# A macaron transformer block on one core: another order of work in the two FP4-quantised feed-forward stages

## What is computed

```
x = x + 0.5 * _L0_ffn_ref(_layernorm(x, axis=-1), ...)      # ffn_a
x = x + _L0_attn_ref(_layernorm(x, axis=-1), ...)           # proj_a, attn_a
x = x + 0.5 * _L0_ffn_ref(_layernorm(x, axis=-1), ...)      # ffn_b
x = x + 0.5 * _L1_ffn_ref(_layernorm(x, axis=-1), ...)      # fp4_a
x = x + _L1_attn_ref(_layernorm(x, axis=-1), ...)           # proj_b, attn_b
x = x + 0.5 * _L1_ffn_ref(_layernorm(x, axis=-1), ...)      # fp4_b
```

```
scale = jnp.max(jnp.abs(xb), axis=-1, keepdims=True) / 6.0
xn = xb / scale
idx = jnp.searchsorted(_MID, jnp.abs(xn))
q = _GRID[idx] * jnp.sign(xn) * scale
...
gate = fp4_linear(x, w_gate)
y = fp4_linear(x, w_up)
h = jax.nn.silu(gate) * y
return fp4_linear(h, w_down)
```

## Time and profile before

| | us |
|---|---|
| median of 3 runs | 526.15 |
| lowest, highest | 522.24, 529.05 |
| the profiled execution | 523.24 |
| its span | 521.4 |
| PE busy | 420.8 (81%) |
| DVE busy | 349.1 (67%) |
| POOL busy | 306.6 (59%) |
| ACT busy | 285.9 (55%) |
| granted TensorE clock, mean | 0.91 |

### The profile page before, as it was taken

One profiled execution on the slowest core, in us unless ns is written; L12 is line 12 of the kernel. 1 busy time (PEld: TensorE's weight loads), 2 busy tenths in 40 slices (PEclk: granted clock), 3 DMA queues, 4 the chain that ended last, 5 costly groups with the idle time before them and its releaser, 6 DMA issues. The chain is left out here.

```text
span 521.4 us, 11437 instructions
## 1 busy us (share of the span) xinstructions
PE 420.8 (81%) x3693; PEld 272.6 (52%) x3693; DVE 349.1 (67%) x882; ACT 285.9 (55%) x521; POOL 306.6 (59%) x585
## 2 busy tenths in 40 slices
PE   3997889999999966945677577899999997567766
PEld 1454436666666533523455354677766774235545
DVE  5768686878888527836677755757677773268771
ACT  5774515676666737657664125245554557567631
POOL 5414435777777732356985423456666668589841
PEclk9999858999999989987999689679999999679995
DMA  6002783233331000000000007943333310000001
GB/s 189 2 1 78 181 247 88 73 80 91 94 92 48 3 1 0 2 1 1 0 1 3 0 27 169 257 103 94 94 96 92 92 50 3 0 2 0 21 27 34
DMA packets 31121, 31.77 MB, mean 61 GB/s; under 512 B 4953, under 2 KB 26329, under 8 KB 31074
## 3 DMA queue, kind: packets, MB, share of 16 engines
q1 hardware_dynamic: 31074, 31.18, 22.6%
HBM read 21.30 MB, written 9.44 MB: 59 GB/s over the span
## 5 line engine op out<-in xcount | busy, mean ns | idle before, releaser
L688 ACT ACTIVATE h_sb<-psum 128x1024 f32<-128x1024 f32 (+1 forms) x128 | 110.8, 914 | 53.1 <-PE psum L614 26.9
L729 DVE TENSOR_REDUCE nm<-psum 128x2 f32<-128x512 f32 x128 | 82.3, 685 | 14.1 <-PE psum L594 12.8
L732 DVE TENSOR_REDUCE nm<-psum 128x3 f32<-128x384 f32 x128 | 66.0, 553 | 10.4 <-PE psum L600 8.1
L698 POOL TENSOR_TENSOR h_sb<-h_sb,bandw 128x512 f32<-128x512 f32 x48 | 61.0, 1271 | 0.0
L234 POOL TENSOR_TENSOR rstd<-veps,mhalf 128x4 f32<-128x4 f32 (+1 forms) x32 | 28.4, 889 | 43.2 <-DVE veps L220 41.8
L1029 PE MATMUL psum<-wgT,fxT 128*128 128x352 f32 x64 | 26.8, 547 | 26.6 <-ACT fxT L1094 26.6
L639 PE MATMUL psum<-h_sb,v_b 128*32 128x256 f32 x512 | 43.2, 410 | 4.2 <-POOL h_sb L698 4.1
L702 POOL TENSOR_SCALAR_AFFINE_SELECT h_sb<-h_sb 128x512 f32<-128x512 f32 x64 | 40.8, 638 | 0.0
L766 DVE RECIPROCAL rsum<-psum 128x16 f32<-128x16 f32 x32 | 8.2, 258 | 46.7 <-PE psum L655 46.7
L593 PE MATMUL psum<-kst,qst 72*128 72x256 bf16 x128 | 36.1, 299 | 3.5 <-DVE nm L729 2.7
L594 PE MATMUL psum<-kst,qst 72*128 72x256 bf16 x128 | 36.0, 298 | 0.0
(11 more groups left out here) (234 smaller groups left out, 1167.5 us busy)
## 6 DMA issues: line engine op xcount, KB each, us to landing
qst<-q_dram SPq DMA_DIRECT2D x96, 96.0 KB
kst<-k_dram SPq DMA_DIRECT2D x96, 96.0 KB
q_dram<-q_parts SPq DMA_DIRECT2D x16, 192.0 KB, 2.9
k_dram<-k_parts SPq DMA_DIRECT2D x16, 192.0 KB, 2.9
k_dram<-k_parts SPq DMA_DIRECT2D x16, 128.0 KB, 3.4
x<-in_L_attn_x SPq DMA_DIRECT2D x4, 256.0 KB, 3.9
out_x<-x SPq DMA_DIRECT2D x4, 256.0 KB, 2.3
pk<-in_packed SPq DMA_DIRECT2D x1, 689.5 KB, 5.7
```

The lines of the kernel that those rows point to most:

```text
L688: nc.scalar.activation(pexp[p][:, :, 0:w], psum[:, 4 + 2 * (p % 2):6 + 2 * (p % 2), 0:w], ACT.Exp, scale=scale).then_inc(sem("a_exp"), 1)
L698: ins = nc.gpsimd.tensor_tensor(wide, wide, bandw[:].unsqueeze(1).unsqueeze(1).to_broadcast([P, 2, 2, P]), ALU.mult)
L729: nc.vector.tensor_reduce(nm[slot % 2][:, HEAD[h]], bank[e].rearrange("p (t k) -> p t k", t=2), AX.X, ALU.max, negate=True).then_inc(sem(" ...
L732: nc.vector.tensor_reduce(nm3[slot % 2][:, HEAD[h]], bank[e][:, 0:3 * P].rearrange("p (t k) -> p t k", t=3), AX.X, ALU.max, negate=True).t ...
```

## The change

The same instructions are issued, with the same shapes, in another order. `pe_f` is parted into transpose, gate and up; `act_f` into the copy of the transposed x and silu; `pool_x_round` into three; h itself is parted from `dve_h_scales`. The steps of a unit get other lags: the chain of x runs ahead, h comes at lag 5, the last x at lag 8, so a stage has 16 steps. fp4_a's steps 0 to 3 stand beside ffn_b's steps 3 to 5, its steps 13 to 15 beside proj_b's 0 to 2; fp4_b's steps 0 to 3 stand before the four slots of the last quad. The weights are quantised with units 4, 5 and 6 of ffn_b, that is in its steps 1, 2 and 3. A few waits on semaphores are added where the new order needs one, such as `wait(pool, "xt", u)`.

```diff
             def pool_x_scaled(pool, u, par):
                 pool.wait_ge(sem("xrs"), u + 1)
+                wait(pool, "xt", u)
...
             def dve_body(dve, k, par, there):
-                if there(4):
-                    dve_h_scales(dve, k - 4, par)
-                if there(5):
-                    dve_h_round(dve, k - 5, 1 - par)
-                if there(1):
-                    dve_x_scales(dve, k - 1, 1 - par)
                 if there(0):
                     dve_stats(dve, k, par)
+                if there(2):
+                    dve_x_scales(dve, k - 2, par)
+                if there(5):
+                    dve_h(dve, k - 5)
+                if there(8):
+                    dve_x(dve, k - 8)
+                if there(5):
+                    dve_h_scales(dve, k - 5, 1 - par)
                 if there(6):
-                    dve_x(dve, k - 6)
+                    dve_h_round(dve, k - 6, par)
 
             def pool_body(pool, k, par, there):
-                if there(2):
-                    pool_x_round(pool, k - 2, par)
                 if there(4):
-                    pool_h_scaled(pool, k - 4, par)
-                if there(5):
-                    pool_h_back(pool, k - 5, 1 - par)
-                if there(1):
-                    pool_x_scaled(pool, k - 1, 1 - par)
+                    pool_x_rounded(pool, k - 4)
+                if there(3):
+                    pool_x_scaled(pool, k - 3, 1 - par)
+                if there(4):
+                    pool_x_back(pool, k - 4, par)
+                if there(6):
+                    pool_h_scaled(pool, k - 6, par)
+                if there(7):
+                    pool_h_back(pool, k - 7, 1 - par)
                 if there(0):
                     pool_rstd(pool, k, par)
+                if there(3):
+                    pool_x_shift(pool, k - 3)
...
-                          ("pe", 1): [("a_y", 8), ("a_exp", PR * 16)]}, {4: 0, 6: 1, 7: 2})
+                          ("pe", 1): [("a_y", 8), ("a_exp", PR * 16)]}, {4: 0, 5: 1, 6: 2})
...
             def next_fp4(slot):
-                if slot >= 2:
-                    step(eng, which, fp4_b, slot - 2)
+                step(eng, which, fp4_b, slot)
...
-            both(ffn_b, 3, 6, fp4_a)
+            for k in range(3):
+                step(eng, which, ffn_b, 3 + k)
+                run(fp4_a, (0, 2, 3)[k], (2, 3, 4)[k])
...
-            run(fp4_a, 3, 11)
+            run(fp4_a, 4, 13)
             proj_b["ahead"](eng, which)
-            both(fp4_a, 11, 14, proj_b)
+            both(fp4_a, 13, 16, proj_b)
             entrance(proj_b, attn_b)
             attention(attn_b, next_fp4)
-            run(fp4_b, 2, 14)
+            run(fp4_b, 4, 16)
```

More of the change, by code:

```diff
@@ L1019, in fp4_phase, with pe_x_transpose @@
             tile_blocks = NBX // 2
[L1021 removed]
+            def pe_x_transpose(pe, u, par):
                 pe.wait_ge(sem("xo"), u + 1)
@@ L1026, in pe_f, with pe_gate @@
                 last.then_inc(sem("d_xTps"), 1)
+            def pe_gate(pe, u, par):
                 pe.wait_ge(sem("d_xT"), u + 1)
@@ L1030, in pe_f, with pe_up @@
                 last.then_inc(sem("d_gps"), 1)
+            def pe_up(pe, u, par):
                 wait(pe, "d_h", u)
@@ L1170, in pool_x_scaled, with pool_x_shift, pool_x_rounded, pool_x_back @@
                 pool.wait_ge(sem("xrs"), u + 1)
+                wait(pool, "xt", u)
                 nc.gpsimd.tensor_tensor(blocks(xbuf["v"][:]), xpad[par][:, :, 0:BLK], spread(xbuf["rs"][:], NBX), ALU.mult).then_inc(sem("xv"), 1)
-            def pool_x_round(pool, u, par):
+            def pool_x_shift(pool, u):
                 pool.wait_ge(sem("xM"), u + 1)
+                wait(pool, "xo", u)
                 nc.gpsimd.tensor_tensor(xbuf["t"][:], xbuf["v"][:], xbuf["M"][:], ALU.add).then_inc(sem("xt"), 1)
+            def pool_x_rounded(pool, u):
                 pool.wait_ge(sem("xt"), u + 1)
                 nc.gpsimd.tensor_tensor(xbuf["t"][:], xbuf["t"][:], xbuf["M"][:], ALU.subtract).then_inc(sem("xq"), 1)
+            def pool_x_back(pool, u, par):
                 pool.wait_ge(sem("xq"), u + 1)
@@ L1205, in pool_body @@
                     pool_rstd(pool, k, par)
+                if there(3):
+                    pool_x_shift(pool, k - 3)
             def pe_body(pe, k, par, there):
-                if there(6):
-                    pe_o_transpose(pe, k - 6, par)
-                if there(3):
-                    pe_f(pe, k - 3, 1 - par)
-                if there(6):
-                    pe_o(pe, k - 6, par)
-            def act_body(act, k, par, there):
-                if there(2):
-                    act_x_magic(act, k - 2)
+                if there(5):
+                    pe_up(pe, k - 5, 1 - par)
@@ new lines, in pe_body, with act_body @@
+                if there(4):
+                    pe_x_transpose(pe, k - 4, par)
+                if there(8):
+                    pe_o(pe, k - 8, par)
+                if there(4):
+                    pe_gate(pe, k - 4, par)
+                if there(7):
+                    pe_o_transpose(pe, k - 7, 1 - par)
+            def act_body(act, k, par, there):
+                if there(3):
+                    act_x_magic(act, k - 3)
+                if there(4):
+                    act_x_copied(act, k - 4, par)
+                if there(1):
+                    act_center(act, k - 1, 1 - par)
+                if there(2):
+                    act_x_six(act, k - 2)
+                if there(6):
+                    act_h_square(act, k - 6, par)
@@ L1218, in act_body @@
                 if there(1):
                     act_scale(act, k - 1, 1 - par)
-                if there(6):
-                    act_o(act, k - 6, par)
-                if there(3):
-                    act_f(act, k - 3, 1 - par)
                 if there(4):
-                    act_h_square(act, k - 4, par)
-                if there(1):
-                    act_x_six(act, k - 1)
-                if there(0):
-                    act_center(act, k, par)
+                    act_silu(act, k - 4)
@@ L1231, in fp4_phase @@
+                if there(7):
+                    act_o(act, k - 7, 1 - par)
             return dict(pe=pe_body, act=act_body, dve=dve_body, pool=pool_body, first=d0, n=8, entry=entry)
@@ L1395, in both @@
                 for k in range(lo, hi):
-                    if ph is not fp4_a or k < 13 or which != "dve":
+                    if ph is not fp4_a or k < 15 or which != "dve":
                         step(eng, which, ph, k)
```

17 lines of the change are left out of this document (9 added, 8 removed).

## The result

| | before | after |
|---|---|---|
| median, us | 527.49 (4 runs) | 507.96 (4 runs) |
| lowest, highest | 522.24, 529.05 | 505.34, 509.61 |
| profiled execution, its span | 523.24, 521.4 | 506.44, 504.6 |
| PE, DVE, ACT, POOL busy in it | 420.8, 349.1, 285.9, 306.6 | 418.7, 350.3, 285.1, 305.0 |
| granted clock, mean | 0.91 | 0.91 |

The ratio is 0.965, with an interval from 0.960 to 0.971: the kernel is faster by 3.5%. The forecast was 509 us for the median and 506.0 for the profiled execution. Busy times are the same within 2.1 us on every engine, so nearly all of the 16.8 us came out of waits. Medians are over all executions of a kernel; every ratio, and a second median where one stands in brackets, leaves out those more than 1.5% above their kernel's fastest.

The account below looks back on a forecast made before the run. Bound: ACT standing still during gate, then PE waiting for ACT. Terms: -8.2 us up to the scores, -9.0 after, so 523.24 profiled becomes 506.0 (0.967), median 509; own range 504 to 514, outer 502 to 519.

Parts of the forecast that it names:

- The ring: Old quantised-stage round: ACT stands still during gate, then PE waits for nearly a round of ACT's work; 6.49 us end to end.
- k = 8 to 10: New rounds of a quantised stage in which POOL, without rstd work, closes the round: 5.25 us.
- The full round: Round k = 7, once a stage, closed by POOL with all its operations: 6.16 us.
- The ring of 4.88: Rounds k = 11 and 12: POOL's h_back, DVE's reduce, reciprocal, scale and roundings, then the next h_back; 4.88 us.
- The weights: ffn_b: weight quantising moved to steps 1 to 3 stalls step 2, +3.1 us; four ready x steps leave gate(0) 0.9 later.
- Attention: Last quad, with fp4_b's steps 0 to 3: attention ends 3.8 us later (bounds 1.2 and 5), gate(0) only 2.1 later.
- The joint: First stage into proj_b: first transposes at 289.4, x(6) 298.0, x(7) 307.4, first scores 317.0 against 325.25, -8.2 us.
- The held-back part: Joint with proj_b: POOL waits some 4 us for proj_b's statistics behind h_round(6); 4.1 of 7.8 us are left.
- The second stage: Gate(0) 454.2, x(4) 495.0 against 502.11, x(4) to x(7) 14.2 against 16.1 us; end -9.0 us.
- POOL's full round as the pace: Rival, chance 0.12: every quantised-stage round takes POOL's 6.16 us, so no gain there; kernel 527 us.
- The clock: Rival, chance 0.05: short PE waits drop its clock to 1.2 GHz, 4.2 us more a round; up to 576 us.
- Another wait puts the old ring back: Rival, chance 0.03: another ACT wait, such as d_h ahead of silu, restores rounds of 6.1 to 6.5; 526 to 532 us.

Follow-up runs that it names:

- The old places: Kernel after, both quantised stages' steps put back where they stood before, new orders kept: 513.85 us; with only the second stage's put back: 509.05 us.
- kernel after's repetition: Kernel after, unchanged, run again beside later kernels on one chip: 510.03 us (508.28), ratio to before 0.964.
- the kernel with both edits: Kernel after, weights back in ffn_b's steps 1, 3 and 4, and proj_b's first DVE statistics one step earlier: 503.95 us, ratio to before 0.957.
- the one with the norm ahead: The kernel with both edits, plus proj_b's step 0 (xn, next statistics) on DVE ahead of quantised step 13: 504.11 us (503.74).
- the last experiment: Same run as the one with the norm ahead: 504.11 us (503.74).

## Why the prediction was right

**The ring.** That ACT stands still under gate while PE waits for ACT was the right mechanism for the old round. Right too are the rounds of the layout: 5.25 forecast for k = 8 to 10, 5.23 and 5.22 measured; 4.8 to 4.88 for the last, 4.76; 3.5 and 4.3 in the filling, 3.41 and 4.71. The full round was given as POOL's 6.16 and is 6.88, with POOL busy 6.72. That was a misreading: 6.92 was called the fullest round before, but the one of 7.20 with POOL busy 6.71 was left out. Gate(0) to gate(1) was to be 5.4 and took 4.61 in the first stage and 5.52 in the second. These misses cancel by luck: the layout had x(0) at 20.4 and it came at 20.23. The ring of 4.88 is also summed from 1.35 and 1.77 where the earlier trace rows has 1.39 and 1.81, which gives 4.96. Gate(0) to x(4): 40.8 forecast, 40.19 and 40.85 measured. Nor do the bounds named add up to the outer range of 502 to 519; added, they reach from 503.3 to some 523.

**What the prediction did not say** is that its two causes only work together. It listed the chain run ahead and ACT's order side by side; undoing silu's place alone takes most of the gain away, and moving silu alone in the kernel before brings none. Its sum was right since it laid out both.

**The weights.** +3.1 for step 2 was right (3.0), and its cause was not (DVE's queue, and xn held by POOL's work on the weight, not POOL's rstd). Gate(0) was to be 0.9 later and came at 236.97, 1.4 later than the earlier trace rows; counted from ffn_b's step 1 it is 28.73 before and 30.41 after, 1.7 later. The four x steps that "stand ready" cover only part: without the move gate(0) would have been 1.0 earlier than before (27.76).

**Attention.** Gate(0) from the scores was to be 2.1 later and is 3.2 later. The term was too small by 1.1, within its bounds; in three other traces with the new places and an early clock it is 2.2 to 2.8 (129.07 to 129.63 us), so a part of the 1.1 is scatter. The last of attention's exps starts 116.87 us behind the scores before and 121.33 after, 4.5 later: 3.8 was forecast, and 5 would have been a sign of being wrong. The old places take 1.75 to 2.4 of it away.

**The joint.** First transposes 289.4 forecast, 289.62 measured; x(6) 298.0 and 298.59; x(7) 307.4 and 307.06; scores 317.0 and 316.51. The held-back part came as described: POOL waited 4.94 us where some 4 were forecast.

**The second stage.** x(4) to x(7) 14.2 forecast, 14.02 measured, and scores to the last x 8.03 us shorter against 9.0: attention's term, 1.1 too small, is all of the missing 1.0.

**The rivals.** POOL's full round as the pace fell: it occurs once a stage. The clock stayed at 1.00 in the rounds behind the first (windows above), with the short waits that the prediction named. The section of the Trainium skill cited there ("TensorE: Matmul & The Clock Gate", "A second HAM failure mode: psum-queue depth-cycling") tells of a bf16 kernel whose clock goes down and up with such idle times; the kernel after does not show it. The kernel before does, though the prediction says that its rounds do not: 0.77 over the round 464.90 to 472.40, which took 7.50 us against 7.20 for the same round of the first stage at 1.00. In the ten traces with the whole new order, silu late, no round behind the first is under 1.00; in each of the four others at least one is. So the new order went with a clock kept up as well, which the forecast did not count. "Another wait puts the old ring back" resembles what happens to each half of the change when made alone, for 526 to 532 there: they took 527.8, 529.6 and 527.1, though the first of them, with rounds of 5.2 to 7.8 us, is not the old ring of 6.1 to 6.5.

## What to carry to other kernels

An engine that waits for a long instruction of another needs two things: a place in its queue for other work ahead of what waits, and other work whose inputs are ready by then. Either alone can measure as nothing, so a software pipeline must be judged with the lag of the steps and the order inside a step changed together. When several edits are made at once, look for the one that only costs: here the weights' earlier steps gave back 2.65 us up to gate(0) and the statistics behind the last rounding 2.4, and undoing both brought 5.6 us from ffn_b's step 1 to the scores. When a round is read, list all of them: the one left out here was the fullest.

## What the runs showed of the hardware

The clock comes up at two moments in attention, in one and the same kernel. Windows of the kernel after and of its repetition, from about 24 to 36 us behind the first scores:

```profile
340.51:352.51 12.00, 11.72 (x177) 8.88 (x174) 8.66 (x21) 6.39 (x12) 7.35 (x23) 1.00 0.30 88
```

```profile
341.20:353.20 12.00, 11.65 (x122) 8.08 (x123) 6.40 (x14) 3.89 (x8) 4.84 (x15) 0.67 0.20 52
```

PE is busy equally long and does 177 matmuls in the one and 122 in the other, at a granted clock of 1.00 and 0.67. From the scores to gate(0) it is then 130.07 us and 133.67; the other kernels with the new places fall on one side or the other in the same way (129.1 to 129.6, and 134.5 to 135.6), also on one and the same chip (the kernel with both edits early; the kernel after's repetition and the one with the norm ahead late). The five traces with the second stage's old places, at 126.7 to 128.3, are all on the early side, which may be chance: this stretch lies ahead of the steps that were moved. A second such place is the start of ffn_b: over 186 to 206 us the clock was 0.91 in the kernel after's repetition and 0.60 in the kernel with old places, and step 1's transposes came at 206.83 and 210.04. A third is the tail. The six executions of the kernel after's repetition lie between 505.47 and 514.37 us, those of the kernel before beside them between 521.65 and 529.69: a spread of 8 to 9 us, which these places would account for, and wider than most of the edits tried here, and this is why stages were compared and not only medians. What decides the moment these runs do not show.

The second thing is DVE beside POOL. The four xn instructions, 1.11 us alone, took 2.45 beside POOL's work on the weights and 2.17 beside POOL's h in the last experiment. Taken one by one, in ffn_b's step 1 of the kernel after, the second and the third of them and the two of POOL are

```profile
204.22 1.03 POOL L997 TENSOR_TENSOR hb_t<-hb_t,hb_v 128x384 f32<-128x384 f32 x1 [0.50 <-DVE hb_t L984]
204.32 1.02 DVE L228 TENSOR_SCALAR xn<-x,mv,rstd 128x128 f32<-128x128 f32 x1
205.26 0.99 DVE L228 TENSOR_SCALAR xn<-x,mv,rstd 128x128 f32<-128x128 f32 x1
205.33 0.84 POOL L1001 TENSOR_TENSOR wgn<-hb_t,wb_sc 128x384 f32<-128x384 f32 x1
```

and one of them without POOL, in step 2 of the kernel with both edits, is

```profile
211.19 0.34 DVE L228 TENSOR_SCALAR xn<-x,mv,rstd 128x128 f32<-128x128 f32 x1
```

The second xn ends less than 0.1 us behind POOL's L997, and the third less than 0.1 behind L1001. The first, which began 0.16 us before L997, and the fourth, behind both, take 0.34 each. The two that were held are longer by 0.68 and 0.65, which is nearly the whole difference between 2.45 and 1.11. In the last experiment one xn of 1.41 us ends less than 0.1 behind POOL's 1.42 of h. The Trainium skill ("SBUF — State Buffer", section "SBUF: two separate sides") says that VectorE and GpSimd share a pair of ports which one instruction holds whole, the other waiting, where the one of VectorE is in a mode with two ports or has two inputs in SBUF. The trace agrees with the waiting. Which of the two conditions xn meets no run shows, nor why the third xn, which by these records began 0.07 us ahead of L1001, was held.
